# Embedding the first batch alone, and scaling the third head's probabilities on VectorE, in a fused attention and expert layer

## What is computed

```python
h = concat([patches @ W.T + b, txt], axis=1)
x = layernorm(h)
q, k, v = x @ Wq.T, x @ Wk.T, x @ Wv.T            # 3 heads of 64
s = (q @ k.T / 8) * decay                         # gamma_head ** (m - l) for m >= l, else 0
o = groupnorm(softmax(s) @ v)                     # mean and variance per batch and head
h = h + (o * gn_weight + gn_bias) @ Wo.T
x = layernorm(h); p = softmax(x @ router.T); top 8 of 16, renormalised
h = h + sum_e p_e * (gelu(x @ w1_e) @ w2_e)       # 8 experts of width 128, 8 of 256
```

## Time and profile before

| | before |
|---|---|
| median of 3 runs | 795.08 us |
| the profiled execution, its time | 794.4 us |
| its span, first to last instruction | 792.1 us |
| TensorE busy (matmul) | 744.4 us, 94% |
| VectorE, ScalarE, GpSimd busy | 551.0, 485.9, 155.8 us |
| mean granted TensorE clock | 0.981 |

### The profile page before, as it was taken

The page is one execution under the profiler, slowest core; times in us unless marked ns, Lnnn a source line. Parts: engine busy times, 40 slices in busy tenths (PEclk is TensorE's granted clock), DMA queues, the critical chain, the costliest instruction groups (busy, mean ns, idle before and its releaser), DMA issues.

```text
span 792.1 us, 13238 instructions
## 1 busy us (share of the span) xinstructions
PE 744.4 (94%) x4400; PEld 635.0 (80%) x4400; DVE 551.0 (70%) x1548; ACT 485.9 (61%) x1087; POOL 155.8 (20%) x261
## 2 busy tenths in 40 slices
PE   6688898999988999999999999999999999999997
PEld 2577787888886777788888888888888888888885
DVE  5588888889788676576567566576666666665654
ACT  1368897897886846456556456556465564564443
POOL 2034436535542780010010010010000100100000
PEclk9689999999998999999999999999999999999999
DMA  7500010011031462242242241342241332412410
GB/s 223 167 2 21 21 42 22 23 42 43 2 100 41 121 184 60 77 127 72 58 115 69 77 128 39 86 125 55 78 120 52 86 104 62 109 62 70 113 50 19
DMA packets 44390, 60.74 MB, mean 77 GB/s; under 512 B 4018, under 2 KB 37762, under 8 KB 44322
## 3 DMA queue, kind: packets, MB, share of 16 engines
q1 hardware_dynamic: 44322, 59.91, 26.5%
HBM read 51.84 MB, written 8.05 MB: 76 GB/s over the span
## 4 chain that ended last, share of the span: by engine, by line
PE 71%; ACT 12%; DVE 7%; issue 4%; POOL 3%; DVEq 1%; POOLq 1%; DMA 0%; SPq 0%
PE ps L1271 67%; ACT pt L595 3%; ACT pr L674 3%; DVE sc L982 2%; ACT ot L595 2%; ACT pr L642 1%; ACT k_hi L595 1%; DVE pr L1006 1%; PE ps L1400 1%; POOL w_lo L553 1%; PE ps L1451 1%; DVE nm L989 1%; ACT xa_hi L595 1%; DVE k_lo L945 1%; POOLq L552 1%
## 5 line engine op out<-in xcount | busy, mean ns | idle before, releaser
L1177 DVE TENSOR_TENSOR act<-act,gate 128x480 f32<-128x480 f32 (+1 forms) x216 | 144.8, 671 | 115.8 <-ACT act L788 110.7
L1271 PE MATMUL ps<-x,w_hi 128*128 128x480 f32 (+1 forms) x648 | 217.0, 389 | 0.2 <-ACT act L788 0.2
L788 ACT ACTIVATE act<-ps 128x480 f32<-128x480 f32 (+1 forms) x216 | 123.7, 573 | 130.2 <-PE ps L1271 130.1
L1271 PE MATMUL ps<-x,w_lo 128*128 128x480 f32 (+1 forms) x432 | 165.9, 384 | 0.0
L945 DVE TENSOR_TENSOR act_lo<-act,act_hi 128x480 fp32r<-128x480 f32 (+1 forms) x216 | 145.0, 671 | 0.2
L1271 PEld LDWEIGHTS ps<-x,w_hi 128*128 128x128 f32 x648 | 121.6, 188 | 21.2 <-ACT act L788 0.7
L595 ACT ACTIVATE act_hi<-act 128x480 fp32r<-128x480 f32 (+1 forms) x216 | 130.7, 605 | 6.8 <-DVE act L1177 6.7
L1271 PEld LDWEIGHTS ps<-x,w_lo 128*128 128x128 f32 x432 | 81.2, 188 | 13.4
L1271 PE MATMUL ps<-act_hi,w_hi 128*128 128x480 f32 (+1 forms) x216 | 83.5, 387 | 4.5 <-DVE act_lo L945 4.5
L1271 PE MATMUL ps<-act_hi,w_lo 128*128 128x480 f32 (+1 forms) x216 | 82.5, 382 | 0.0
L1271 PE MATMUL ps<-act_lo,w_hi 128*128 128x480 f32 (+1 forms) x216 | 82.5, 382 | 0.0
(11 more groups left out here) (181 smaller groups left out, 1257.0 us busy)
## 6 DMA issues: line engine op xcount, KB each, us to landing
gate<-comb_dram SPq DMA_DIRECT2D x112, 240.0 KB, 3.2
gate<-comb_dram SPq DMA_DIRECT2D x32, 256.0 KB, 3.8
w_raw<-w SPq DMA_DIRECT2D x16, 384.0 KB, 3.7
h_dram<-h SPq DMA_DIRECT2D x8, 384.0 KB
res<-h_dram SPq DMA_DIRECT2D x7, 360.0 KB, 4.4
out<-res SPq DMA_DIRECT2D x7, 360.0 KB, 3.2
h<-txt SPq DMA_DIRECT2D x3, 672.0 KB
decay_rows<-drow SPq DMA_DIRECT2D x1, 1014.0 KB, 8.4
```

Of the source, the lines that this page charges most:

```text
L788: a.activation(act[j % 3][:, 0:n], ps[:, up_bank(j), 0:n], ACT.Gelu_apprx_tanh).then_inc(gelu_done, 1)
L1177: dve.tensor_tensor(act[j % 3][:, 0:n], act[j % 3][:, 0:n], gate[e % 4][:, 0:n], ALU.mult).then_inc(gated, 1)
L1271: return pe.matmul(dst, w, x, start=start, stop=stop)
```

## The change

**Start.** The host hands over the patches of batch 0 (`first_patches`) apart from the others. SP's order becomes: patches of batch 0, both halves of `tokw`, text of batch 0, the q and k columns of the attention weights, the other patches, the other columns, the group norm's constants, the decay table's store and load, text of batch 1, w1, text of batches 2 to 7. PE embeds 36 columns (12 matmuls), transposes them, and then does the first 128 features of the other 252 columns; the other 64 features follow inside batch 0, between its two blocks of scores, and the transposes of batches 1 to 7 in four groups after that. DVE's doubling is cut into three stretches, and the split of the attention weights into two.

**Attention.** `scale_probs` is gone, and `normalise` scales five tiles for every head. The third head's output is copied once, into 64 partitions (`Y_ROWS`). The statistics of batch b + 2 are taken after q and k (`norm_parts`) and joined after the third head's decay (`norm_join`). `qk` makes k's tile second, and `scores_pair` waits for the rests of the first two tiles alone, with a wait for the others ahead of tile 2. `o_copy(t, 1)` moves behind the copies of the next batch's first two tiles. The three parts of `add_attention` stand together after `normalise(b, 1)`. All bank tables change.

**Last batch and first expert tile.** `project(5)` moves from the body's end to where the other bodies have it, the router's steps move behind `probs_transpose(7, 0)`, ACT does the last exponentials before the copy of the gates, `up(0)` and `up(1)` move ahead of and behind `comb_transpose`, and the third head of batch 7 is transposed in one step.

```diff
@@ SP: loads @@
+            sp.dma_start(pat[:, :, 0:IMG], first_patches).then_inc(ld_pat[0], 16)
             for i in range(2):
                 part = slice(i * KT // 2, (i + 1) * KT // 2)
-                sp.dma_start(pat[:, part, :], patches[:, part, :]).then_inc(ld_pat[i], 16)
                 sp.dma_start(tokw[:, part, :], tok_w[:, part, :]).then_inc(ld_pat[i], 16)
             sp.dma_start(tokb[:, :], tok_b).then_inc(ld_pat[1], 16)
             load_h(0, 1, ld_h0)
-            sp.dma_start(aw_raw[:, :, :], attn_w).then_inc(ld_aw, 16)
-            load_h(1, B, ld_h)
-            sp.dma_start(w1_raw, w1[:, :, 0:W1_SHARE]).then_inc(ld_w1, 16)
+            sp.dma_start(aw_raw[:, :, 0:QK_W], attn_w[:, :, 0:QK_W]).then_inc(ld_aw[0], 16)
+            sp.dma_start(pat[:, :, IMG:B * IMG], patches).then_inc(ld_pat[2], 16)
+            sp.dma_start(aw_raw[:, :, QK_W:AW], attn_w[:, :, QK_W:AW]).then_inc(ld_aw[1], 16)
...
             sp.dma_start(decay[:, :, :], shifted[:, :, 0:L]).then_inc(ld_decay, 16)
+            load_h(1, 2, ld_h1)
+            sp.dma_start(w1_raw, w1[:, :, 0:W1_SHARE]).then_inc(ld_w1, 16)
+            load_h(2, B, ld_h)
@@ ACT: body @@
                 qk_round(b, 0)
                 qk_round(b, 1)
                 if tail:
-                    scale_probs(t)
-                for part in (2, 3):
-                    qk_round(b, part)
+                    o_copy(t, 1, O_BANKS[1])
+                qk_round(b, 2)
+                qk_round(b, 3)
...
-                exps(b, 0)
+                exps(b, 0, (0, 1))
+                if not tail:
+                    a.wait_ge(emb_done, 3)
+                    embedded(emb[0:HD, 1, IMG:B * IMG], ps[0:HD, IMG_REST, 0:(B - 1) * IMG], 1).then_inc(emb_copied, 1)
+                exps(b, 0, (2, 3, 4))
@@ DVE: normalise, body @@
-                for I in range(2 if hh == 2 else 0, NT):
+                for I in range(NT):
...
                 if tail and ahead:
-                    dve.wait_ge(ln1_rstd, nth(b, 1, 2))
-                    norm_stats(b + 2, st6, mv, veps, ln1_var)
+                    norm_parts(b + 2, st6)
...
                 apply_decay(b, 0)
                 apply_decay(b, 1)
+                normalise(b, 0)
                 if not tail:
+                    dve.wait_ge(ld_h1, 16 * NT)
+                    image_tokens(1)
+                    image_tokens(2)
+                    dve.drain()
                     norm_stats(1, st6, mv, veps, ln1_var)
-                normalise(b, 0)
                 apply_decay(b, 2)
...
+                if tail and ahead:
+                    dve.wait_ge(ln1_rstd, nth(b, 1, 2))
+                    norm_join(st6, mv, veps, ln1_var)
                 normalise(b, 1)
...
+                if later:
+                    add_attention(b - 2, WO_BANKS)
@@ PE: start, scores_pair @@
+            embed(0, 0, 0, IMG)
+            embed(1, 1, 0, IMG).then_inc(emb_done, 1)
             pe.wait_ge(emb_copied, 1)
             pe.wait_ge(consts, 2)
...
+            image_transpose(0)
+            pe.wait_ge(ld_pat[2], 16)
+            embed(0, 0, IMG, B * IMG).then_inc(emb_done, 1)
...
-                pe.wait_ge(qk_lo, nth(b, 4, 4))
+                pe.wait_ge(qk_lo, nth(b, 4, 2))
```

More of the change, by code:

```diff
@@ L130, in nth, with early_fusion @@
     return b * per + k
-def early_fusion(nc, patches, txt, tok_w, tok_b, gammas, gn_w, gn_b, attn_w, w1, w2, out):
+def early_fusion(nc, first_patches, patches, txt, tok_w, tok_b, gammas, gn_w, gn_b, attn_w, w1, w2, out):
     ctx = ExitStack()
@@ L367, in body @@
                     load_w2(1)
-                if later and more:
+                if later:
                     store_h(b - 2)
@@ L701, in o_copy @@
                 for half, n in enumerate(ATTEND_W):
-                    for p in ((0,), (HD,), (0, HD))[hh]:
-                        last = copy(ot[b % 2][p:p + HD, hh // 2, at:at + n], ps[HD * half:HD * half + HD, bank, 0:n])
+                    p = HD * (hh % 2)
+                    last = copy(ot[b % 2][p:p + HD, hh // 2, at:at + n], ps[HD * half:HD * half + HD, bank, 0:n])
                     at += n
@@ L756, in body @@
                 v_copy(b, (2,))
-                if not more:
-                    x2_round(0, 0, 5)
-                    x2_round(0, 1, 4)
                 exps(b, 1, (2, 3, 4))
@@ L931, in _ @@
             norm_join(st6, mv, veps, ln1_var)
-            for i in range(1, B // 2):
-                last = image_tokens(i)
-            last.then_inc(embt_copied, 1)
+            decay_powers(256, L - 1).then_inc(decay_built, 1)
             norm_share(0, rstd, nmr, ln1_rstd, xn, first_normed)
+            weights_lo(0)
             for t in (0, 1):
@@ L1134, in body @@
                 apply_decay(b, 1)
+                normalise(b, 0)
                 if not tail:
+                    dve.wait_ge(ld_h1, 16 * NT)
+                    image_tokens(1)
+                    image_tokens(2)
+                    dve.drain()
                     norm_stats(1, st6, mv, veps, ln1_var)
-                normalise(b, 0)
                 apply_decay(b, 2)
-                if later and more:
-                    add_attention(b - 2, WO_BANKS, (0,))
-                if not more:
-                    x2_rest(0, 0, 5)
-                    x2_rest(0, 1, 4)
+                if tail and ahead:
+                    dve.wait_ge(ln1_rstd, nth(b, 1, 2))
+                    norm_join(st6, mv, veps, ln1_var)
                 normalise(b, 1)
-                if later and more:
-                    add_attention(b - 2, WO_BANKS, (1, 2))
                 if not tail:
+                    image_tokens(3)
+                    image_tokens(4)
+                    dve.drain()
+                if later:
+                    add_attention(b - 2, WO_BANKS)
+                if ahead and not tail:
+                    dve.wait_ge(ld_h, 16 * NT)
                     dve.wait_ge(ln1_rstd, 2)
@@ L1164, in body @@
                 normalise(b, 2)
-                if not more:
-                    add_attention(b - 2, LAST_WO[b - 2])
             x_ext(0)
             x_lo(0)
+            weights_lo(1)
             iterations(body)
@@ L1307, in x_transpose @@
                 for c in range(2):
+                    if c == 0 and b >= 3:
+                        pe.wait_ge(wo_added, nth(b - 3, 3, 3))
                     if c == 1 and b:
@@ L1316, in qk @@
                 for i in range(3):
-                    tile, bank = (0, 2, 1)[i], QK_BANKS[i]
+                    tile, bank = i, QK_BANKS[i]
+                    if i == 0 and not tail:
+                        pe.wait_ge(aw_lo_ready, 1)
                     if i == 0 and tail:
                         pe.wait_ge(o_copied, nth(b - 1, 3, 1))
+                        pe.wait_ge(pt_copied, nth(b - 1, 4 * H, 4 * 2))
                     ah, al, bh, bl = weights(tile * P, (tile + 1) * P)
```

368 lines of the change are left out of this document (199 added, 169 removed).

## The result

Before: 795.66 us (median of 4 runs on this chip, 794.88 to 797.28). After: **783.28 us** (median of 4, 782.83 to 783.79). The ratio is 0.9836, 95% interval 0.982 to 0.9853: 1.6% faster. The profiled execution took 783.68 us with a span of 781.9; before it was 792.1. The forecast was 776.5 us, from 767.5 to 788.

What follows compares the result with a forecast made beforehand. TensorE, busy 94%, was taken as the bound, with gains only in its idle or slow-clock time. From 794.4, less 8.3, 6.0 and 4.2, came 775.9; with the median 0.7 higher, 776.5 us was predicted, range 767.5 to 788.

Steps and rivals of the forecast that it cites:

- The likeliest case: Whole kernel: the forecast of 776.5 us itself, given 0.58, with its own range of 771 to 782 us.
- my first rival: Start gives half: half clock through batch 0, table or text late; start 4, loop 3, end 2.5 us; 785; chance 0.22.
- The start: Up to the first scores: a single chain whose links move, scores at 26.1 instead of 37.8 us, 11.7 us earlier.
- Batch 0: First batch: 3.4 us longer from image copies and the embedding's rest; start and batch 0 together -8.3 us.
- The loop: Attention periods: VectorE takes over the beat, 27.04 us instead of 28.04; six periods give -6.0 us.
- it has 26.4 us of work in 28.0: Attention loop: VectorE's work per period, read from its waits of 0.90 and 0.72 us; nearly full.
- The rule weighed in the prediction: VectorE and GpSimd share a port pair exclusively, exposing two more scalings; nothing added in the loop.
- my estimate by one meeting per batch: Loop: lock met once in each of seven batches at 1.08 us, sum 7.6 us higher, 784.
- The hand-over: Last batch into first expert tile: earlier products and fewer waits, -4.2 us, bounds 0 and -7.
- comes at 269.7: Hand-over: first `down` product at 269.7 instead of 270.50 us, half the third head's transposes already done (0.9 us).
- about 2 us of later waits go: Hand-over: w2 and the gates behind it on SP's queue arrive earlier, saving about 2 us of waits.
- Earlier exponentials let GpSimd start on w2 some 4.9 us earlier: Hand-over: reason given for w2 and gates arriving earlier and about 2 us of later waits going.

Runs made afterwards that it cites:

- start_rest_first: Changed kernel with TensorE's twelve 252-column products for the other batches put back ahead of the transposes of batch 0's image tokens: 790.35 us, ratio 0.9925.
- start_text_first: Changed kernel with the text of batches 1 to 7 issued ahead of the decay rows' store and load, as before the change: 792.31 us, ratio 0.9948.
- loop_w1_halving_late: Changed kernel with GpSimd's halving of the batch's w1 share put back behind the power for the batch after next: 779.85 us, ratio 0.9785.
- end_up_products_twice: Changed kernel with the first three up products of the first expert tile computed twice each: 781.37 us, ratio 0.9809.
- end_reordered: Changed kernel with the w1 halving late and the whole hand-over reordered on VectorE, GpSimd, TensorE and ScalarE: 780.45 us, ratio 0.9794.
- end_reordered_up_twice: The kernel of end_reordered with the second up product computed twice, in TensorE's gap before the scaled probabilities: 780.15 us, ratio 0.9794.

## Why the prediction was right, and where it was not

**Direction and range: right.** 783.3 lies in 767.5 to 788, and faster had 0.92. The likeliest case's own range, 771 to 782, was missed by 1.3 us; the measured time lies at my first rival's 785, but not by its mechanism: that had the start giving half and the clock low in batch 0.

**The start: right link by link, and better in the last.** Forecast and measured: first matmul 5.2 and 5.04, image copy 11.0 and 10.88, transposes 17.3 and 17.01, projections 20.1 and 19.68. The scores then took 5.0 us instead of 6.0, under my lower bound of 5.4, with TensorE at full clock (6.6 us in start_rest_first, where it was not): 24.7, not 26.1. The patches' wait of 1.40 us and wide products of 5.41 instead of 4.7 us were not in the sum. The transposes stood right behind them, while the normalised tokens were ready at 16.1, not at 16.8; the two slips and the 0.5 us I had added cancelled. The decay rows were in time, as start_text_first shows by taking that away.

**Batch 0: right.** 23.1 us instead of 20.3, so 2.8 more where I had 3.4. Start and batch 0: -10.3 us for a forecast of -8.3.

**The loop: right mechanism, one term mis-sized.** VectorE took over the period and the scalings took 1.60 us. The period came out at 27.4 us in four cases, 28.2 and 26.8 in one each, not 27.04: -3.6 us for -6.0. The failed step is "it has 26.4 us of work in 28.0". I took that from one period, and in that one GpSimd happened to cost VectorE little. Before the change, in batches 3 and 4 (VectorE, beside the `xa_lo` at 170.67 in the earlier trace rows):

```profile
134.54 1.00 DVE L989 TENSOR_SCALAR nm<-mx 128x4 f32<-128x4 f32 x1
...
142.46 0.76 DVE L945 TENSOR_TENSOR xa_lo<-ps,xa_hi 128x580 fp32r<-128x580 f32 x1 [0.29 <-ACT xa_hi L595]
...
162.75 0.33 DVE L989 TENSOR_SCALAR nm<-mx 128x4 f32<-128x4 f32 x1
```

The negation took 0.33 us in batch 4, and 0.99 to 1.01 us in the six other batches from 1 to 7. Counted from one `xa_lo` to the next, VectorE has 26.6 us of work in batch 4 (waits of 0.90 and 0.72 us) and 27.0 in batch 3 (0.90 and 0.29), and both take 28.2 us. So while ScalarE set the period, the meeting was paid out of VectorE's wait for `xa_hi` and cost nothing. Once VectorE sets the period, it is on the path. The changed kernel has it in each of the six periods. In four of them it costs 0.6 us. In the first and the sixth VectorE waits for TensorE (0.95 and 1.20 us), and there taking it away won nothing. From the 27.0 us of batch 3 my sum would have been 27.6. Measured were 27.4 with the meeting and 26.8 with the halving late, so the other moves saved VectorE more than the 0.2 us I gave them; which of them did was not separated. With the halving late the six periods are 27.07 us in the mean and give 5.8 us. That this is the forecast's 6.0 is in part luck, since no period has that length: four are 26.8 and two 27.6 and 27.7. The changed kernel's one period of 28.2 us has another cause: there the third head's scalings took 2.06 us, behind 0.43 us in which VectorE waited for nothing that the profile shows, and with the halving late they did the same (2.06 and 0.44).

The rule weighed in the prediction, the Trainium skill, SBUF — State Buffer, section "SBUF: two separate sides" (an exclusive lock between VectorE and GpSimd), was set aside because the scalings did not run under GpSimd's wide work. In the kernel it bears on another instruction than in my text: one meeting a batch, at 0.85 us on VectorE, and loop_w1_halving_late agrees with it (0.17 us instead of 1.02 once GpSimd's work is elsewhere). That my estimate by one meeting per batch was 784 us is no proof: the late halving gives back only 2.2 us between batches 1 and 7, and the rest of my error is the hand-over.

**The hand-over: wrong, in sign.** Forecast -4.2 us, measured +3.7 (H from 90.1 to 93.8). The failed step is that the first `down` product "comes at 269.7", and that "about 2 us of later waits go". In distances from `xa_hi` of batch 7, I had the first `down` product at 43.4 us for 44.2 before; it came at 46.8. I had summed TensorE's work and let the rest follow. Two things took it. The gates go out 38.7 us after `xa_hi` of batch 7 instead of 37.3: the router's chain did not come earlier relative to the batch, and TensorE's moved-up products only opened waits in front of it. And the lower clock covered the first `down` product and the `up` product behind it, where a matmul of 512 columns took 0.63 instead of 0.40 us. end_up_products_twice and start_text_first put this at 2.8 us of the 3.7, each by one trace. That is what the changed kernel would win back, and not a cost that the kernel before was free of: its clock was at 0.66 from 250 to 260 us, ahead of its first `up` product. The remaining 0.9 us are 1.9 us more up to the first `down` product and 1.0 us less behind it.

The reason I gave for the later waits failed too: "Earlier exponentials let GpSimd start on w2 some 4.9 us earlier". GpSimd, before and after:

```profile
264.12 0.51 POOL L550 CAST w_hi<-w_raw 128x384 fp32r<-128x384 f32 x1 [1.75 <-ACT pr L674]
```

```profile
246.07 1.01 POOL L458 TENSOR_TENSOR rstdb<-vepsb,neg_half 128x4 f32<-128x4 f32 x1 [9.90 <-DVE vepsb L1086]
...
250.50 0.67 POOL L553 CAST w_hi<-w_raw 128x384 fp32r<-128x384 f32 x1
```

It starts on w2 37.8 us after `xa_hi` of batch 7 before and 38.1 after. The exponentials, done at 246.6, no longer hold it: it is busy with the second tile's norm, for which it waited 9.90 us for VectorE's statistics. The fifth gate still goes out 1.5 us earlier than before (46.6 for 48.1).

**Sum.** -10.3 - 3.6 + 3.7 = -10.2 us of span, for a forecast of -18.5. That the range held owes something to luck: the start was 2.0 us better than forecast, the loop 2.4 and the hand-over 7.9 us worse, and the last is outside its own bounds of 0 and -7.

## What to carry to other kernels

Before sizing an engine's work from one period, read the same instruction in every period: a tiny operation that takes 0.17 us in one and 1.02 us in the next may be meeting another engine, and when its engine comes to set the period that meeting is on the path. Work moved up on the busiest engine pays only as far as what it hands to moves too; follow the chain (here router, DRAM, gate, and the transfer queued behind a buffer) to its own bound before counting a gain. And a start that is one chain is shortened only as a whole: here the order of the transfers and the order of the products were each needed.

## What the runs showed of the hardware that I had not expected

- A VectorE operation on 128x4 elements, 0.17 us alone, took 1.02 us when it fell on GpSimd's subtraction of 128x384 elements. Its length does not protect it: it lost 0.85 us, where the five wide scalings lost 0.25 us in the meeting with the halving (1.82 for 1.57).
- Computing three products twice made the kernel no slower (781.37 for 783.28 us, intervals that overlap), and its profiled span 3.5 us shorter (778.4 instead of 781.9), 2.8 us of it in the hand-over. On top of the late halving it won nothing.
- In end_reordered and end_reordered_up_twice the clock fell once more, in batch 1: the transposes that take 1.83 us took 3.39 and 3.14 us, after waits of 1.83 and 1.82 us. In loop_w1_halving_late, whose loop is the same, they took 1.83 us after a wait of 1.84 us. The period of batch 1 was 28.96, 28.95 and 27.66 us. So the same code with the same wait met either clock.
- Executions with the same start differ by up to 2.2 us already at the first `xa_hi` (17.31 to 19.49 us), so places in two traces are best compared as distances from a common instruction.
